# The last mixture of a two-layer kernel, computed with weight rows stationary instead of token rows

## The chip, the cores and the metric

The kernel is one program on one core of a Trainium2 chip. The metric is the device time of one execution in microseconds (us). Three executions of the kernel before took 1348.96, 1352.48 and 1351.76 us, median 1351.76.

## What is computed

A stream of 2048 tokens of 256 numbers (8 sequences of 256) goes through two layers. Each layer is a gated cross-attention to a short context and a gated mixture of experts. The change touches only the mixture of the second layer: 8 experts and a shared MLP of twice the width, so that 10 blocks of 176 hidden numbers (1760 in all) are computed for every token. The reference's second mixture comes down to this (its text is cut to what it computes; `combine` is zero for the experts that a token did not choose and one for the two shared blocks):

```python
xn = layernorm(x)                                   # [2048, 256]
p = softmax(xn @ gate_weight.T)                     # 8 experts
combine = where(p is among its row's two largest, p, 0), then two columns of 1
g, u = xn @ gate_rows.T, xn @ up_rows.T             # [2048, 1760] each
h = silu(g) * u * repeat(combine, 176, axis=1)
x = x + g_ffn[1] * (h @ down)                       # down [1760, 256]
```

The two products with `gate_rows` and `up_rows` are each made of three products of rounded halves (high by high, high by low, low by high), in the format fp32r.

## The kernel before

Tokens are handled in NG = 4 groups of G = 4 tiles of P = 128 tokens. The five engines run their own instruction lists and meet at semaphores. PSUM banks are used in rings of two: `q_ring` (products that VectorE reads), `s_ring` (products that ScalarE reads), `t_ring` (transposes and small products that ScalarE copies out), and the two `o_banks` for the final sums. A `fill` on TensorE waits until the bank's former content was read; a `read` waits until the bank is full.

The mixture of a group (`mixture` at lines 1214, 1527 and 1963 for VectorE, ScalarE and TensorE) works tile by tile:

- `gates_ups(j)` (products at line 1978): for each of 5 pairs of blocks, six products into an `s_ring` bank (gate) and six into a `q_ring` bank (up). The 128 tokens of the tile are stationary and 352 weight columns move. That is 60 products a tile and 240 a group.
- ScalarE applies Silu to each gate bank (line 1536, `sg`), 128 by 352. VectorE multiplies `sg`, the up bank and the token's combine weight in one instruction for each block (line 1208). Since tokens lie on the partitions, the combine weight is a scalar for each partition.
- `down(j)`: the 1760 hidden numbers lie along the free axis, so 14 transposes (line 1989) bring them onto partitions, four ScalarE copies (line 1541, `attnT`) take them out of PSUM, and 14 fp32 products of 256 columns (line 1997) sum them against `dn1` in one `o_bank`. Each such product appears in the trace as two instructions. `residual` (line 648) adds the sum to x.

TensorE's order in a group is gates_ups 0, gates_ups 1, down 0, gates_ups 2, down 1, gates_ups 3, the front of the next group, down 2, down 3. The front (`mixture_front`) transposes the next group's normalized tokens (line 1611), waits for ScalarE's four copies (lines 1449 and 1450), and computes the 8 gate logits (line 1876). VectorE's `gating` (lines 1187 to 1198) makes the combine weights from the logits. In its middle it waits for an exponential of ScalarE (line 1458). It runs after the last tile's multiplications. Groups 0 to 2 are one hardware loop, group 3 stands behind it. When all is done, SyncE stores the whole x (2 MB) at line 454.

Of the kernel before, what the change touches and what calls it, by code (L numbers as in the profile page):

```python
# [6 lines left out]
F32R = mybir.dt.float32r  # L7
I32 = mybir.dt.int32
ACT = mybir.ActivationFunctionType
ALU = mybir.AluOpType  # L10
# [18 lines left out]
W1 = (E1 + 2) * F1  # L29
# [72 lines left out]
def flamingo(nc, a, out, stages=4):  # L102
    with ExitStack() as ctx:
# [3 lines left out]
        def sem(name):  # L107
# [93 lines left out]
        gu_hi = sb("gu_hi", [P, 2 * G * ROW + 2 * NA * G * DIM + T // 2 + 2 * DIM], F32R)[:, 0:C * 5 * 4 * F1].rearrange(  # L201
            "p (c e g n) -> p c e g n", c=C, e=5, g=2)
# [17 lines left out]
        gu1 = sb("gu1", [P, C, 5, 2, 2 * F1], scope=loaded)  # L220
        loaded.close()
        gu_lo = sb("gu_lo", [P, C, 5, 2, 2 * F1], F32R)
        dn1 = sb("dn1", [P, FC, DIM])
        gate1 = sb("gate1", [P, C, E1])
        sg = sb("sg", [P, 2, 2 * F1])
        combine_w = sb("combine_w", [P, G, E1 + 2])
        act_v = soft[:].rearrange("p j n -> p (j n)")[:, 0:2 * FC * P].rearrange("p (b n) -> p b n", b=2)
# [13 lines left out]
        xnT_hi, xnT_lo = (xnT_split[:, n * C * G * P:(n + 1) * C * G * P].rearrange("p (c t) -> p c t", c=C)  # L241
                          for n in range(2))
# [89 lines left out]
        gate_exp = sem("gate_exp")  # L332

# [19 lines left out]
        QM, SM, TM, TMF = 20, 20, 20, 4  # L353
# [4 lines left out]
        def _(sp):  # L358
# [86 lines left out]
            sp.dma_start(gu1[:], a["L1_gu"].rearrange("(c p) e g n -> p c e g n", p=P)).then_inc(w4_loaded, 16)  # L445
# [5 lines left out]
            with sp.Fori(1, NG - 1) as i:  # L451
                next_context(i)
            sp.wait_ge(x_done, 1)
            sp.dma_start(out_d, x[:]).then_inc(stored, 16)
            sp.wait_ge(stored, 16)

        @block.gpsimd
        def _(pool):
# [99 lines left out]
            key_blocks(NG - 1)  # L558

        @block.vector  # L560
        def _(dve):
# [514 lines left out]
            def split_weights(p):  # L1076
                dve.wait_ge(w_rounded, p + 1)
                dve.tensor_tensor(gu_lo[:, :, p], gu1[:, :, p], gu_hi[:, :, p], ALU.subtract).then_inc(w_split, 1)

            def split_xn(i):  # L1080

                dve.wait_ge(xn_rounded, i + 1)
                dve.tensor_tensor(xnT_lo, xnT[:], xnT_hi, ALU.subtract).then_inc(xn_split, 1)
# [92 lines left out]
            GATE_CHAIN = 5 + 6  # L1176

            def gating(i):
# [7 lines left out]
                dve.wait_ge(t_ring.free, T5 + TMF - 8 + TM * i)  # L1186
# [12 lines left out]
                ch.wait()  # L1199

            def products(i, j):

                for p in range(5):
                    dve.wait_ge(s_ring.free, S5 + SM * i + 5 * j + p + 1)
                    b = qr.read(dve)
                    for e in range(2):
                        at = (2 * p + e) * F1
                        ins = dve.scalar_tensor_tensor(  # L1208
                            out=act_v[:, j % 2, at:at + F1], in0=sg[:, (j + p) % 2, e * F1:(e + 1) * F1],
                            scalar=combine_w[:, j, 2 * p + e:2 * p + e + 1], in1=b[:, e * F1:(e + 1) * F1],  # L1210
                            op0=ALU.mult, op1=ALU.mult)
                    ins.then_inc(q_ring.free, 1)

            def mixture(i, last):
                ch.at(MIX_BASE + MIX_CHAIN * i)
                qr.at(Q5, QM, i)
                products(i, 0)
                if not last:
                    row_stats(i + 1)
                products(i, 1)  # L1220
                if not last:
                    row_roots(EPS0)
                residual(3 * NG + i, 0, i, 3)
                if not last:

                    row_apply(i + 1)
                products(i, 2)
                residual(3 * NG + i, 1, i, 3)
                products(i, 3)
                if not last:  # L1230
                    split_xn(i + 1)
                    gating(i + 1)
                residual(3 * NG + i, 2, i, 3)
                residual(3 * NG + i, 3, i, 3)
                assert last or ch.k == MIX_CHAIN, ch.k
# [8 lines left out]
            with dve.Fori(0, NG - 1) as i:  # L1244
                mixture(i, False)
            mixture(NG - 1, True)
# [3 lines left out]
        def _(act):  # L1250
# [195 lines left out]
            def mixture_front():  # L1446
                for c in range(C):
                    b = tr.read(act)
                    act.activation(xnT_hi[:, c, :], b[:], ACT.Copy)
                    act.activation(xnT[:, c, :], b[:], ACT.Copy).then_inc(t_ring.free, 1)  # L1450
# [9 lines left out]
            def attention(i, last):  # L1460
# [18 lines left out]
                def round_weights(p):  # L1479
                    act.activation(gu_hi[:, :, p], gu1[:, :, p], ACT.Copy).then_inc(w_rounded, 1)  # L1480
# [3 lines left out]
                if last:  # L1484
                    mixture_front()
                    act.wait_ge(w4_loaded, 64)
# [39 lines left out]

            def mixture(i, last):
                sr.at(S5, SM, i)
                tr.at(T5 + TMF, TM, i)

                def silu(j):
                    for p in range(5):
                        b = sr.read(act)

                        act.wait_ge(q_ring.free, Q5 + QM * i + 5 * j + p - 1)
                        act.activation(sg[:, (j + p) % 2, :], b[:, 0:2 * F1], ACT.Silu).then_inc(s_ring.free, 1)  # L1536

                def act_out(j):
                    for g in range(4):
                        n = min(4, FC - 4 * g)  # L1540
                        act.activation(attn_flat[:, 4 * g:4 * g + n, :], tr.read(act)[:, 0:n * P].rearrange(  # L1541
                            "p (f t) -> p f t", f=n), ACT.Copy).then_inc(t_ring.free, 1)

                silu(0)
                silu(1)
                act_out(0)
                silu(2)
                act_out(1)
                silu(3)
                if not last:  # L1550
                    mixture_front()
                act_out(2)
                if not last:
                    gate_exponential(i + 1)
                act_out(3)

            attn_flat = attnT[:].rearrange("p b f t -> p (b f) t")
            gate_exponential(0)
            with act.Fori(0, NG - 1) as i:
                mixture(i, False)  # L1560
            mixture(NG - 1, True)

        @block.tensor
        def _(pe):
# [399 lines left out]

            def mixture(i, last):
                qr.at(Q5, QM, i)
                sr.at(S5, SM, i)
                tr.at(T5 + TMF, TM, i)

                def gates_ups(j):  # L1970
                    for p in range(5):
                        for o, (ring, end) in enumerate(((s_ring, sr), (q_ring, qr))):
                            b = end.fill(pe)

                            terms = [(v, w, c) for c in range(C) for v, w in (
                                (xnT_hi, gu_hi), (xnT_hi, gu_lo), (xnT_lo, gu_hi))]
                            for n, (v, w, c) in enumerate(terms):
                                mm = pe.matmul(b[:, 0:2 * F1], v[:, c, j * P:(j + 1) * P], w[:, c, p, o, :],  # L1978
                                               start=(n == 0), stop=(n == len(terms) - 1))
                            mm.then_inc(ring.full, 1)  # L1980

                def down(j):

                    pe.wait_ge(q_ring.free, Q5 + QM * i + 5 * (j + 1))
                    for g in range(4):
                        b = tr.fill(pe)
                        for f in range(4 * g, min(4 * g + 4, FC)):
                            n = min(P, W1 - f * P)
                            mm = pe.transpose(b[0:n, (f % 4) * P:(f % 4 + 1) * P],  # L1989
                                              act_v[:, j % 2, f * P:f * P + n], ident[:])  # L1990
                        mm.then_inc(t_ring.full, 1)
                    pe.wait_ge(o_read, G * (3 * NG + i) + j + 1)
                    for f in range(FC):
                        n = min(P, W1 - f * P)
                        if f % 4 == 0:
                            tr.evacuated(pe, 4 - f // 4)
                        mm = pe.matmul(o_banks[j % 2][:, 0:DIM], attn_flat[0:n, f, :], dn1[0:n, f, :],  # L1997
                                       start=(f == 0), stop=(f == FC - 1))
                    mm.then_inc(o_full, 1)

                pe.wait_ge(xn_split, i + 1)
                gates_ups(0)
                gates_ups(1)
                down(0)
                gates_ups(2)
                down(1)
                gates_ups(3)
                if not last:
                    mixture_front(i + 1)
                down(2)  # L2010
                down(3)

            attn_flat = attnT[:].rearrange("p b f t -> p (b f) t")
# [45 lines left out]
```

## Time and profile before

| what | value |
|---|---|
| executions | 1348.96, 1352.48, 1351.76 us (median 1351.76) |
| the profiled execution | 1348.91 us, its span 1347.2 us |
| mean granted TensorE clock over the span | 0.833 |
| TensorE products, busy share of the span | 77% |
| VectorE, ScalarE, GpSimd, busy share | 53%, 32%, 22% |
| stretch of the last mixture | 1034.4 to 1338.7 us |
| VectorE busy in it | about a third of each group or less |

The span runs from the first to the last instruction; the time of the execution is 1.7 us longer. The profile lists for each engine when it was busy, what ended its idle times, and the chain of work that ended last. Durations of matmuls overlap their neighbours in the record, so what a product costs is read from the distance between starts, or from the chain, and not from its own duration. The granted clock is 1.00 at 2.4 GHz and 0.50 at 1.2 GHz.

### The profile page before, as it was taken

The numbers are of one execution on the slowest core, as the hardware profiler recorded it, in microseconds if no ns is written. First come the engines' busy times: TensorE is split into PE (matmuls) and PEld (weight loads), VectorE is DVE, ScalarE is ACT, GpSimd is POOL, SyncE is SP. The second block draws the span as 40 slices with busy tenths as digits, with TensorE's granted clock in tenths as the row PEclk, the third lists the DMA queues.
The fourth block names the chain that finished last, engine by engine and source line by source line (L and its number), as shares of the span: only waits on it lengthen the run. The fifth ranks groups of instructions, "written<-read, shape, count | busy, mean of one in ns | idle before, by whom it ended". The sixth has DMA issues, their size and how long they took to land. (4 is left out here: it accounts for less than half of the span.)

```text
span 1347.2 us, 16347 instructions
## 1 busy us (share of the span) xinstructions
PE 1040.4 (77%) x5301; PEld 860.9 (64%) x5301; DVE 714.3 (53%) x1663; ACT 428.9 (32%) x789; POOL 296.6 (22%) x231
## 2 busy tenths in 40 slices
PE   5989989999766500866775447878879999999997
PEld 3857858678554300755665226564757989899896
DVE  6367586674768896222222488575865424242221
ACT  4555365544623100111111032323252232322321
POOL 0414223133000001788787120120200000000000
PEclk9999999999877655877778666767676999999999
DMA  7004000000001140788886620000000000000001
GB/s 264 3 0 136 1 1 1 0 1 1 0 0 39 42 108 22 168 182 175 170 175 113 191 107 1 2 0 0 0 0 0 1 1 0 0 0 0 0 0 63
DMA packets 59495, 66.39 MB, mean 49 GB/s; under 512 B 5565, under 2 KB 56247, under 8 KB 58679
## 3 DMA queue, kind: packets, MB, share of 16 engines
q1 hardware_dynamic: 45796, 46.52, 11.1%
q0 software_dynamic: 12288, 18.88, 7.9%
q8 instruction: 28, 0.46, 0.1%
q10 hardware_dynamic: 1363, 0.37, 0.1%
q14 instruction: 20, 0.16, 0.0%
HBM read 48.16 MB, written 17.56 MB: 49 GB/s over the span
## 5 line engine op out<-in xcount | busy, mean ns | idle before, releaser
L1978 PE MATMUL bank<-gu_hi,xnT_split 128*128 128x352 f32 x640 | 159.4, 329 | 0.0
L476 POOL TENSOR_TENSOR q_lo<-soft,q_hi 128x512 fp32r<-128x512 f32 x64 | 93.1, 1455 | 238.0 <-ACT soft L1338 237.8
L1978 PEld LDWEIGHTS bank<-gu_hi,xnT_split 128*128 128x128 f32 x640 | 113.4, 191 | 1.0 <-issue 0.7
L487 POOL DMA_INDIRECT xg<-table,src_now x64 | 63.9, 999 | 217.6 <-DVE src_now L948 198.5
L497 POOL DMA_INDIRECT acc<-y,dst_now x64 | 102.2, 1596 | 26.7 <-issue 20.6
L1978 PE MATMUL bank<-gu_lo,xnT_split 128*128 128x352 f32 x320 | 104.2, 326 | 0.0
L1208 DVE SCALAR_TENSOR_TENSOR soft<-sg,combine_w,bank 128x176 f32<-128x176 f32 x160 | 56.5, 394 | 88.1 <-PE bank L1978 82.3
L1997 PE MATMUL bank<-dn,attnT 128*128 128x256 f32 x448 | 102.1, 387 | 0.0
L1997 PEld LDWEIGHTS bank<-dn,attnT 128*128 128x128 f32 x448 | 86.1, 195 | 11.5
L728 DVE COPY qT<-bank 128x512 f32<-128x512 f32 x64 | 44.2, 690 | 89.3 <-PE bank L1683 88.2
L1536 ACT ACTIVATE sg<-bank 128x352 f32<-128x352 f32 x80 | 37.1, 464 | 153.0 <-PE bank L1978 153.0
L1783 PEld LDWEIGHTS bank<-xgT,w_gu 128*88 128x88 f32 x512 | 81.2, 205 | 7.1 <-issue 3.8
L1783 PE MATMUL bank<-xgT,w_gu 128*88 128x128 f32 x512 | 83.7, 333 | 0.7 <-issue 0.7
L648 DVE SCALAR_TENSOR_TENSOR x<-bank,gates,x 128x256 f32 (+1 forms) x48 | 22.8, 482 | 115.1 <-PE bank L1997 95.6
L968 DVE TENSOR_SCALAR y<-bank,xg 128x256 f32<-128x256 f32 x64 | 28.0, 479 | 96.5 <-PE bank L1796 79.2
L1769 PE MATMUL bank<-ident,xg 128*128 128x128 f32 x128 | 25.6, 333 | 59.4 <-DMA xg<-table,src_now 59.4
L1334 ACT ACTIVATE q_hi<-qT 128x512 fp32r<-128x512 f32 x64 | 40.4, 631 | 93.1 <-DVE qT L728 93.0
L1638 PE MATMUL bank<-vw,attnT 128*128 128x256 f32 x256 | 61.5, 395 | 4.2 <-ACT attnT L1288 4.2
L1668 PE MATMUL bank<-kT,qT 128*128 128x64 f32 x512 | 64.0, 268 | 0.0
L1668 PEld LDWEIGHTS bank<-kT,qT 128*128 128x128 f32 x512 | 62.5, 191 | 1.5
L1978 PEld LDWEIGHTS bank<-gu_lo,xnT_split 128*128 128x128 f32 x320 | 61.0, 191 | 0.3
L1769 PEld LDWEIGHTS bank<-ident,xg 128*128 128x128 f32 x128 | 17.9, 171 | 64.4 <-DMA xg<-table,src_now 54.1
(255 smaller groups left out, 2165.4 us busy)
## 6 DMA issues: line engine op xcount, KB each, us to landing
w_gu<-in_L_ffn_w_gu SPq DMA_DIRECT2D x32, 352.0 KB
w_dn<-in_L_ffn_w_down SPq DMA_DIRECT2D x32, 176.0 KB
acc<-zeros SPq DMA_DIRECT2D x2, 2176.0 KB, 12.0
acc_rows<-acc SPq DMA_DIRECT2D x8, 512.0 KB, 4.9
gu<-in_L_gu SPq DMA_DIRECT2D x1, 3520.0 KB, 13.3
table<-xw SPq DMA_DIRECT2D x4, 640.0 KB
wo<-in_L_xattn_Wo SPq DMA_DIRECT2D x2, 1024.0 KB, 15.7
wq<-in_L_xattn_Wq SPq DMA_DIRECT2D x1, 2048.0 KB, 18.0
```

Of the source, the lines that this page charges most:

```text
L476: pool.tensor_tensor(q2_lo[:, h % 3, :], q2[h % 2], q2_hi[:, h % 3, :], ALU.subtract).then_inc(q2_split, 1)
L487: pool.indirect_dma_start(xg[:, q, e, :], None, table, bass.IndirectOffsetOnAxis(ap=src_now[:, q, e:e + 1], axis=0)).then_inc(xg_loaded[q] ...
L497: pool.indirect_dma_start(acc[e], bass.IndirectOffsetOnAxis(ap=dst_now[:, q, e:e + 1], axis=0), y[:, q, e, :], None, compute_op=ALU.add).t ...
L728: dve.tensor_copy(qT[:, h % 3, :], qr.read(dve)[:]).then_inc(q_ring.free, 1)
L1208: ins = dve.scalar_tensor_tensor(out=act_v[:, j % 2, at:at + F1], in0=sg[:, (j + p) % 2, e * F1:(e + 1) * F1], scalar=combine_w[:, j, 2 * ...
L1334: act.activation(q2_hi[:, h % 3, :], qT[:, h % 3, :], ACT.Square)
L1638: mm = pe.matmul(o_banks[0][:, 0:DIM], attnT[:, j % 2, p, :], vw[:, j // 2, p, :], start=(p == 0), stop=(p == 7))
L1668: mm = pe.matmul(s_bank[0][:, at:at + SKV], qT[:, h % 3, j * P:(j + 1) * P], kT[:, h, (j // 2) * SKV:(j // 2 + 1) * SKV], start=True, stop ...
L1769: mm = pe.transpose(b[:, at:at + P], xg[:, q, e, c * P:(c + 1) * P], ident[:])
L1783: mm = pe.matmul(b[0:I0, e * P:(e + 1) * P], w_gu[:, q, e, c, o:o + I0], xgT[:, q % 2, e, c, :], start=(c == 0), stop=(c == C - 1))
L1978: mm = pe.matmul(b[:, 0:2 * F1], v[:, c, j * P:(j + 1) * P], w[:, c, p, o, :], start=(n == 0), stop=(n == len(terms) - 1))
L1997: mm = pe.matmul(o_banks[j % 2][:, 0:DIM], attn_flat[0:n, f, :], dn1[0:n, f, :], start=(f == 0), stop=(f == FC - 1))
```

## The change

The second mixture's products are turned around. A group is no longer worked tile by tile but in FC = 14 pieces of 128 hidden rows (the last has 96). For each piece `gate_up(f)` on TensorE makes

- one product of `chooser` (20 rows, the piece's 128 columns, stationary) with `combine_T` (20 rows, 512 tokens moving) into a `q_ring` bank: the combine weight of each hidden row's block, for each token. The 20 rows are the ten combine weights, rounded, and their ten remainders;
- six products into an `s_ring` bank and six into a `q_ring` bank with 128 weight rows stationary and 512 tokens moving.

ScalarE applies Silu to 128 by 512. VectorE multiplies twice over 512 columns, `sg` by the spread combine weights and then by the up bank. The result already has hidden rows on partitions. `down(f)` needs no transposes and is four products of 256 columns, one for each tile, into halves of the two `o_banks`, summed over the 14 pieces. TensorE runs gate_up(f) and then down(f - 1). The front of the next group stands after piece 6. `gating` stands on VectorE after piece 9, with its exponential on ScalarE after the Silu of piece 10. Two operations behind `gating` split the combine weights, and `combine_across` with `combine_in` transpose them for the next group. For group 0 these stand ahead of its first product. `xnT_hi` and `xnT_lo` have two buffers, GpSimd builds `chooser` after its last work, the loops over the groups are written out, and SyncE stores x in four parts of 512 KB as groups end.

```diff
+            def combine_across(i):
+                pe.wait_ge(combine_split, i + 1)
+                for half in range(2):
+                    b = tr.fill(pe)
+                    for k in range(2):
+                        mm = pe.transpose(b[0:2 * NW, k * P:(k + 1) * P], combine_2[:, 2 * half + k, :], ident[:])
+                    mm.then_inc(t_ring.full, 1)
+
             def mixture(i, last):
-                def gates_ups(j): ...
-                def down(j): ...
+                def gate_up(f):
+                    n, at = min(P, W1 - f * P), slice(f * P, min(f * P + P, W1))
+                    pe.matmul(qr.fill(pe)[0:n], chooser[:, at], combine_T[:], start=True,
+                              stop=True).then_inc(q_ring.full, 1)
+                    for g, (ring, end) in enumerate(((s_ring, sr), (q_ring, qr))):
+                        b = end.fill(pe)
+                        terms = [(w, v, c) for c in range(C) for w, v in (
+                            (gu_hi, xnT_hi), (gu_lo, xnT_hi), (gu_hi, xnT_lo))]
+                        for k, (w, v, c) in enumerate(terms):
+                            mm = pe.matmul(b[0:n], w[:, c, g, at], v[i % 2][:, c, :], start=(k == 0),
+                                           stop=(k == len(terms) - 1))
+                        mm.then_inc(ring.full, 1)
+                def down(f):
+                    pe.wait_ge(q_ring.free, Q5 + QM * i + 2 * f + 2)
+                    if f == 0:
+                        pe.wait_ge(o_read, 2 + 3 * NT + G * i)
+                    n = min(P, W1 - f * P)
+                    for j in range(G):
+                        mm = pe.matmul(o_banks[j // 2][:, j % 2 * DIM:(j % 2 + 1) * DIM],
+                                       act_v[0:n, f % 2, j * P:(j + 1) * P], dn1[0:n, f, :],
+                                       start=(f == 0 and j % 2 == 0), stop=(f == FC - 1 and j % 2 == 1))
+                        if f == FC - 1 and j % 2:
+                            mm.then_inc(o_full, 2)
+                tr.evacuated(pe)
                 pe.wait_ge(xn_split, i + 1)
+                for f in range(FC):
+                    gate_up(f)
+                    if f:
+                        down(f - 1)
+                    if f == 6 and not last:
+                        mixture_front(i + 1)
+                if not last:
+                    combine_across(i + 1)
+                down(FC - 1)
 # VectorE
+                ch.add(dve.tensor_copy(combine_2[:, :, 0:NW].bitcast(F32R), combine_w[:]))
+                ch.wait()
+                dve.tensor_tensor(combine_2[:, :, NW:2 * NW], combine_w[:], combine_2[:, :, 0:NW],
+                                  ALU.subtract).then_inc(combine_split, 1)
+            def products(i, f):
+                n, v = min(P, W1 - f * P), act_v[:, f % 2, :]
+                dve.wait_ge(s_ring.free, S5 + SM * i + f + 1)
+                dve.tensor_tensor(v[0:n], sg[0:n, f % 2, :], qr.read(dve)[0:n], ALU.mult).then_inc(q_ring.free, 1)
+                qr.evacuated(dve)
+                dve.tensor_tensor(v[0:n], v[0:n], qr.read(dve)[0:n], ALU.mult).then_inc(q_ring.free, 1)
+                for f in range(FC):
+                    products(i, f)
+                    if not last:
+                        ...
+                        elif f == 8:
+                            split_xn(i + 1)
+                        elif f == 9:
+                            gating(i + 1)
+                mixture_out(i)
 # ScalarE
+                for f in range(FC):
+                    n, b = min(P, W1 - f * P), sr.read(act)
+                    act.wait_ge(q_ring.free, Q5 + QM * i + 2 * f - 3)
+                    act.activation(sg[0:n, f % 2, :], b[0:n], ACT.Silu).then_inc(s_ring.free, 1)
+                    if not last:
+                        if f == 6:
+                            mixture_front(i + 1)
+                        elif f == 10:
+                            gate_exponential(i + 1)
+                if not last:
+                    combine_in()
 # SyncE
+            for i in range(NG):
+                sp.wait_ge(o_read, 2 + 3 * NT + G * (i + 1))
+                sp.dma_start(out_d[:, G * i:G * (i + 1), :], x[:, G * i:G * (i + 1), :]).then_inc(stored, 16)
             sp.wait_ge(x_done, 1)
-            sp.dma_start(out_d, x[:]).then_inc(stored, 16)
-            sp.wait_ge(stored, 16)
+            sp.wait_ge(stored, 16 * NG)
```

## Rows read from the trace of the kernel before

**Rows 1.** Stretches of groups 1 and 3 and the end: busy, clock, DMA

```profile
1114.20:1190.80 76.60, 74.05 (x433) 69.53 (x433) 25.48 (x81) 22.45 (x45) 0.00 (x0) 0.98 0.00 0
...
1267.90:1338.70 70.80, 69.74 (x408) 65.16 (x407) 16.07 (x45) 17.10 (x36) 0.00 (x0) 1.00 0.00 1
1338.70:1347.20 8.50, 0.00 (x0) 0.00 (x0) 0.46 (x1) 0.00 (x0) 0.00 (x0) 0.79 0.74 247
```

**Rows 2.** Chain that ended last, end of group 1: start, us, what

```profile
1159.16 9.60 PE bank L1978 x60
...
1171.43 2.18 PE bank L1876 x16
1173.61 3.05 PE bank L1989 x14
...
1182.71 0.45 PE bank L1989 x4
...
1184.76 6.05 PE bank L1997 x28
```

**Rows 3.** Timeline of TensorE, layer 0 queries, six fp32r products of 512 columns

```profile
211.97 0.39 PE L1683 MATMUL bank<-xnT_rest,wq_hi 128*128 128x512 f32 x1
...
213.13 0.28 PE L1659 MATMUL bank<-q_hi,band_r 128*16 128x256 f32 x1
...
213.59 1.00 PE L1668 MATMUL bank<-kT,qT 128*128 128x64 f32 x8
```

**Rows 4.** Timeline around a product with one row stationary, full clock

```profile
968.83 0.29 PEld L1924 LDWEIGHTS bank<-bo,ones 1*128 1x128 f32 x2 [0.33 <-issue]
968.83 0.69 PE L1924 MATMUL bank<-bo,ones 1*128 1x256 f32 x2
969.45 0.20 PEld L1915 LDWEIGHTS bank<-ident,c 128*128 128x128 f32 x2 [0.33 <-issue]
```

**Rows 5.** Timeline around products with 16 rows stationary

```profile
80.67 1.45 PE L1574 MATMUL bank<-wk,ctxK 128*128 128x512 f32 x3
...
82.05 0.32 PEld L1701 LDWEIGHTS bank<-ident,n_rows 16*128 16x128 f32 x4 [0.76 <-issue]
```

**Rows 6.** Timeline of ScalarE and VectorE in the gating of group 1

```profile
1099.17 1.28 ACT L1458 ACT_TABLE_LOAD   x1
1100.46 0.23 ACT L1458 ACTIVATE gate_s<-gate_s 128x32 f32<-128x32 f32 x1
1100.72 0.18 DVE L1191 TENSOR_REDUCE gate_s<-gate_s 128x4 f32<-128x32 f32 x1 [3.76 <-ACT gate_s L1458]
...
1103.77 0.19 DVE L1198 TENSOR_TENSOR combine_w<-gate_s 128x32 f32<-128x32 f32 x1
```

**Rows 7.** Groups by line: busy us, mean ns, idle before

```profile
L1536 ACT ACTIVATE sg<-bank 128x352 f32<-128x352 f32 x79 | 36.7, 464 | 153.0 <-PE bank L1978 153.0
L1541 ACT ACTIVATE attnT<-bank 128x512 f32<-128x512 f32 x48 | 27.0, 595 | 36.2 <-PE bank L1989 36.2
...
L728 DVE COPY qT<-bank 128x512 f32<-128x512 f32 x64 | 44.2, 690 | 89.3 <-PE bank L1683 88.2
```

**Rows 8.** Timeline before and at the start of the last mixture

```profile
1030.05 0.69 PE L1915 MATMUL bank<-ident,c 128*128 128x128 f32 x2
...
1030.77 0.38 ACT L1476 ACTIVATE c1T<-bank 128x256 f32<-128x256 f32 x1 [5.86 <-PE bank L1915]
...
1038.76 0.19 DVE L1198 TENSOR_TENSOR combine_w<-gate_s 128x32 f32<-128x32 f32 x1
```

**Rows 9.** Stretches of lower clock: busy, granted clock (third from the end)

```profile
1034.40:1039.30 4.90, 4.90 (x18) 4.90 (x18) 3.88 (x15) 1.98 (x3) 0.00 (x0) 0.50 0.00 0
...
1171.00:1176.00 5.00, 4.57 (x28) 4.31 (x28) 1.60 (x3) 1.81 (x5) 0.00 (x0) 0.70 0.00 0
```

**Rows 10.** DMA issues: size, median us from issue to landing

```profile
out<-x SPq DMA_DIRECT2D x1, 2048.0 KB, 7.5
...
cand<-cand SPq DMA_DIRECT2D x1, 32.0 KB, 1.8
```

More of the change, by code:

```diff
@@ L28 @@
 E1, F1 = 8, 176
-W1 = (E1 + 2) * F1
+NW = E1 + 2
+W1 = NW * F1
 FC = -(-W1 // P)
@@ L240, in flamingo @@
         xnT_split = sb("xnT_split", [P, QK * D1 + C * G * P], F32R)
-        xnT_hi, xnT_lo = (xnT_split[:, n * C * G * P:(n + 1) * C * G * P].rearrange("p (c t) -> p c t", c=C)
-                          for n in range(2))
+        xnT_other = sb("xnT_other", [P, 2 * C * G * P], F32R)
+        xnT_hi, xnT_lo = ([v[:, n * C * G * P:(n + 1) * C * G * P].rearrange("p (c t) -> p c t", c=C)
+                           for v in (xnT_split, xnT_other)] for n in range(2))
         qk1_stat = sb("qk1_stat", [P, 2, QK])
@@ L332, in flamingo @@
         gate_exp = sem("gate_exp")
+        chooser_step = sem("chooser_step")
+        chooser_ready = sem("chooser_ready")
+        combine_split = sem("combine_split")
         x_d = a["x"].rearrange("b t d -> (b t) d").rearrange("(n p) d -> p n d", p=P)
@@ L558, in _ @@
             key_blocks(NG - 1)
+            blank = sg[:].rearrange("p b n -> p (b n)")[0:2 * NW, 0:NW // 2 * F1].rearrange(
+                "p (e n) -> p e n", e=NW // 2)
+            for half in range(2):
+                if half:
+                    pool.wait_ge(chooser_ready, half)
+                pool.memset(blank, 0.0).then_inc(chooser_step, 1)
+                for part_ in range(2):
+                    pool.wait_ge(chooser_step, 3 * half + part_ + 1)
+                    pool.affine_select(out=blank, in_=blank, compare_op=ALU.not_equal, fill=1.0,
+                                       base=-NW // 2 * half - NW * part_, pattern=[[-1, NW // 2], [0, F1]],
+                                       channel_multiplier=1).then_inc(chooser_step, 1)
+                pool.wait_ge(chooser_step, 3 * half + 3)
+                pool.tensor_copy(chooser[:, half * NW // 2 * F1:(half + 1) * NW // 2 * F1].rearrange(
+                    "p (e n) -> p e n", e=NW // 2), blank).then_inc(chooser_ready, 1)
         @block.vector
@@ L1199, in gating, with mixture_out @@
                 ch.wait()
[L1201 to L1212, printed above, removed]
+                ch.add(dve.tensor_copy(combine_2[:, :, 0:NW].bitcast(F32R), combine_w[:]))
[8 more added lines that the diff above has]
+                dve.tensor_tensor(v[0:n], v[0:n], qr.read(dve)[0:n], ALU.mult).then_inc(q_ring.free, 1)
+            def mixture_out(i):
+                for j in range(G):
+                    dve.wait_ge(o_full, G * (3 * NG + i) + 2 * (j // 2 + 1))
+                    xj = x[:, G * i + j, :]
+                    dve.scalar_tensor_tensor(out=xj, in0=o_banks[j // 2][:, j % 2 * DIM:(j % 2 + 1) * DIM],
+                                             scalar=gates[:, 3:4], in1=xj, op0=ALU.mult,
+                                             op1=ALU.add).then_inc(o_read, 1)
             def mixture(i, last):
@@ L1216, in mixture @@
                 qr.at(Q5, QM, i)
[L1217 to L1234, printed above, removed]
+                for f in range(FC):
+                    products(i, f)
+                    if not last:
+                        if f == 1:
+                            row_stats(i + 1)
+                        elif f == 2:
+                            row_roots(EPS0)
+                        elif f == 3:
+                            row_apply(i + 1)
+                        elif f == 8:
[3 more added lines that the diff above has]
+                mixture_out(i)
                 assert last or ch.k == MIX_CHAIN, ch.k
@@ L1243, in _ @@
             dve.wait_ge(o_read, 2 + 3 * NT)
-            with dve.Fori(0, NG - 1) as i:
-                mixture(i, False)
-            mixture(NG - 1, True)
+            for i in range(NG):
+                mixture(i, i == NG - 1)
             dve.drain().then_inc(x_done, 1)
@@ L1525, in _, with combine_in @@
             attention(NG - 1, True)
+            def combine_in():
+                for half in range(2):
+                    act.activation(combine_T[:, half * 2 * P:(half + 1) * 2 * P], tr.read(act)[0:2 * NW, 0:2 * P],
+                                   ACT.Copy).then_inc(t_ring.free, 1)
             def mixture(i, last):
                 sr.at(S5, SM, i)
[L1529 to L1549, printed above, removed]
-                if not last:
[L1551 to L1557, printed above, removed]
+                for f in range(FC):
[7 more added lines that the diff above has]
+                            gate_exponential(i + 1)
+                if not last:
+                    combine_in()
             gate_exponential(0)
-            with act.Fori(0, NG - 1) as i:
-                mixture(i, False)
-            mixture(NG - 1, True)
+            tr.at(T5 + TMF)
+            combine_in()
+            for i in range(NG):
+                mixture(i, i == NG - 1)
         @block.tensor
@@ L1967, in mixture @@
                 sr.at(S5, SM, i)
[L1968 to L1999, printed above, removed]
@@ new lines, in down @@
+                def down(f):
[3 more added lines that the diff above has]
+                    n = min(P, W1 - f * P)
+                    for j in range(G):
+                        mm = pe.matmul(o_banks[j // 2][:, j % 2 * DIM:(j % 2 + 1) * DIM],
[3 more added lines that the diff above has]
+                            mm.then_inc(o_full, 2)
@@ L2014, in _ @@
+                down(FC - 1)
             pe.wait_ge(w_split, 5)
-            with pe.Fori(0, NG - 1) as i:
-                mixture(i, False)
-            mixture(NG - 1, True)
+            pe.wait_ge(chooser_ready, 2)
+            tr.at(T5 + TMF)
+            combine_across(0)
+            for i in range(NG):
+                mixture(i, i == NG - 1)
 _INS = ["x", "ctx_1024", "g_xattn", "g_ffn", "L0_xattn_Wq", "L0_xattn_Wk", "L0_xattn_Wo",
```

52 lines of the change are left out of this document (24 added, 28 removed).

## Prediction, made before the changed kernel ran

> **What bounds the kernel now.** I read the busy stretches first, then the chain that ended last, then timelines at the places where the chain changes. In the stretches [rows 1] the reader sees TensorE busy for 74.05 of 76.60 us in group 1 and for 69.74 of 70.80 us in group 3, VectorE for 25.48 and 16.07. So the last mixture, 1034.4 to 1338.7 us, goes by what TensorE executes plus the few places where it waits. The chain says what that is [rows 2]. One tile's 60 gate and up products take 9.60 us, 0.160 each. One `down` takes 2.05 us from its first transpose (1182.71) to its first real product (1184.76), with a wait for ScalarE in it, and then 6.05 us for 14 products in 28 passes, 0.216 a pass. The front of the next group, from the end of the 60 products (1168.76) to the next transposes (1173.61), takes 4.85 us. Four tiles give 4 x (9.60 + 2.05 + 6.05) = 70.8 us, which is group 3, and the front with its slow clock makes 76.6 us of it in group 1. The sum closes, so each of these terms may be exchanged for a new one.
>
> **Removed.** The transposes, with their ScalarE wait: 16 tiles x 2.05 = **-32.8 us** [rows 2].
>
> **Unchanged.** `down` has 56 products of 256 columns a group before and after. The passes of 0.216 us are as many. The front stays as it is.
>
> **The pieces.** A group has 14 x 12 = 168 products with 512 moving columns in place of 240 with 352. The same kind of product stands in the layer 0 queries [rows 3]: from 211.97 to 213.13 lie five of them, 0.232 us each. 672 x 0.232 = 155.6 us against 960 x 0.160 = 153.6: **+2.0 us**. The gain of wider products is nothing; columns set the price (86016 against 84480 a group).
>
> **The spreading product, streaming.** 14 a group with 512 columns: 56 x 0.232 = **+13.0 us**. That only 20 rows are used makes it no shorter: the passes over one row in [rows 4] are no shorter than those over 128 (below).
>
> **The spreading product, its breaks.** Here I look at products whose stationary operand has few rows, among others of 128. In [rows 4] a product over one row begins at 968.83 and the next one's weights at 969.45: 0.62 us for two passes of 256 columns that take 0.43 us in [rows 2]. So 0.19 us is lost. The weight load's idle time ahead of it reads "issue": nothing that the trace shows kept it from being loaded under the matmuls before, as all others are. It began only when these had ended. It is the same on the way in (0.33 us of idle ahead of both). In [rows 5] the products with 16 rows do it too: three matmul passes from 80.67 at 0.43 us each end at 81.96, and the load follows at 82.05, with its own 0.1 us still to come. In [rows 3] the change from 16 columns to 128 (213.13 to 213.59, four passes of 0.115) costs nothing, so it is the rows that do it and not the columns. The chooser has 20 rows, close to 16, and stands alone between products of 128 rows, so it has a break on either side: 2 x 56 x 0.2 = **+22.4 us**. Bounds: 0 if 20 rows behave like 128, and 0.3 us each at the lower clock. I take the 16-row and 1-row value, as 20 is nearest to 16.
> The Trainium skill, page "TensorE: Matmul & The Clock Gate", section "LDWEIGHTS (loading the stationary operand)", says that a load goes by its columns, so that 32 rows take as long as 128. It knows no break, and by it this term would be 0 and the sum +1.8 us. The durations of the loads agree with it, the idle time before them does not, and I go by the latter; the first rival is the page's case.
>
> **The start.** Now TensorE begins the products at 1034.4, while VectorE is still gating until 1038.95 [rows 8], and it runs 4.9 us at clock 0.50 [rows 9]. In the changed kernel the two splitting operations come first (2 x 0.22, to 1039.4), then two transposes (0.69 for two, [rows 8]), then two copies of 0.38 with a hop each, and only then `tr.evacuated` lets the pieces begin: about 1041.0, **+6.6 us**. I let the slow stretch of 4.9 us move with it (bounds: not there, -2.5; twice as long, +2.5). In groups 1 to 3 the four transposes lie in TensorE's list for 0.6 us each time, and the copies hide under down(13), 1.7 us: **+1.9 us**.
>
> **The gating.** This is a new wait, in the middle of a group. VectorE stands in `gating` after piece 9, and queued behind it is its multiplication of piece 10, which alone frees the bank for the spreading product of piece 11. `gating` waits in its middle for an exponential that stands behind the Silu of piece 10. Counted from the end of the gate product of piece 10: Silu 0.07 + 0.60 (464 ns for 352 columns, 595 for a copy of 512, [rows 7]), table load 1.28, exponential 0.23, hop 0.03, VectorE's chain from 1100.72 to 1103.96 = 3.24, the two new operations 0.44, the multiplication 0.03 + 0.69 (a 512 column read of PSUM, [rows 7]), hop 0.06: 6.67 us [rows 6]. In that time TensorE has up(10), 6 x 0.232, and down(9), 8 x 0.216: 3.12 us. It stands still for 3.55 us, in three groups: **+10.7 us**. In the kernel before this chain lay beside down(2).
>
> **The clock.** After a pause the clock falls: the front's wait for four ScalarE copies is followed by 5 us at 0.70 [rows 9], which is 3 us at the lower level and 1.5 us of lost work. The front keeps its own. The gating's pause is longer, so I give it one such loss a group: **+4.5 us** (bounds 0, and two spells each of 1.7, 10.2).
>
> **The rest.** Piece by piece VectorE and ScalarE are covered. Silu ends 0.67 and the first multiplication 1.4 us after the gate product, the second 2.1; TensorE needs the first bank after 1.39 + 1.73 = 3.1 us, and down of the piece some 3 us later. row_stats, row_roots, row_apply and split_xn each fit in the 3 us that a piece leaves on VectorE (row_roots, the longest, is 12 small operations at the 0.22 us steps of [rows 6], 2.6 us); if that cover were gone, each would cost what it is longer than it. GpSimd builds `chooser` after its last work of layer 1, in layer 1's last attention group, with nothing queued behind it; if TensorE came first it would wait at `chooser_ready`. The written-out loops and the second buffers I cost at 0. The end: now the last sum ends at 1338.65, and 8.5 us follow [rows 1], with the 2 MB store landing after 7.5 [rows 10]. After the change two `x` additions in a row (0.5 us more) and a 512 KB store, between 1.8 (32 KB) and 7.5 us, by proportion of size 3.2: **-3.8 us** (bounds -5 and +0.5).
>
> **Sum.** -32.8 + 2.0 + 13.0 + 22.4 + 6.6 + 1.9 + 10.7 + 4.5 - 3.8 = **+24.5 us**. From the profiled execution's own 1348.9 that is 1373.4; from the median of the runs, 2.9 higher, 1376.3. I predict **1375**. What I call the same below is within 0.3%, 4 us, about what a measurement of this kernel can tell from none.
>
> **Rivals.**
> *The chooser has no breaks* (20 rows are handled as 128, or its load is pulled under the passes of down). For it: the 96-row products among the 28 passes of `down` show none (0.216 a pass with them, [rows 2]). Against it: all rows with 1 and 16 rows show one. Sum +2.1, time 1351 to 1354, not slower by what can be told. The point at which it decides is a break of 0.02 us: 112 x 0.02 = 2 us carries the sum over 4 us. Chance 0.12.
> *A product's price is its weight load, not its columns*: a load lasts 0.19 us, and 352 columns run at 0.160. If 512 ran at 0.160 too, 728 products would save 0.072 each, -52 us, time 1323, faster. Against it, [rows 3] have exactly this product at 0.232. Chance 0.02. The Trainium skill, same page, section "Back-to-back issue gap", gives about 131 ns for 512 columns in a stream with loads; by it 728 x 0.1 = 73 us less, 1302. The trace disagrees.
> *The clock falls more often*: each gating pause brings two slow spells and the start stays slow twice as long: +5.7 + 2.5, time 1383. For it: the pause is twice the front's; against it, the front costs one spell. Chance 0.10.
> *As worked out*: 0.76, with its own range 1362 to 1385.
>
> **How the numbers follow.** Low end: forecast from 1348.9 with no clock losses at start and pauses and the best store, 1373.4 - 2.5 - 4.5 - 1.2 = 1365, less a few us for breaks of 0.15: 1361. High end: 1376.3 + 8.2 = 1385, with a dearer store 1387. Outside lie the two cases with chances 0.12 and 0.02 and a few in a hundred above. Faster by over 0.3%: 0.02 from the second, 0.02 from the first and 0.01: 0.05. Same: 0.07, nearly all of the first. Slower: 0.88.
>
> **What would show it.** The last product at about 1367 in the span (1338.7 + 24.5 + 3.8). Weight loads of the chooser and of the first gate product with idle time "issue" ahead of each, 0.62 us from chooser start to gate start; a piece of 5.1 us (4.7 without breaks). Pieces of six products at 0.232. No transposes of `soft`. The first piece at 1041. In groups 0 to 2 one TensorE pause of 3.5 us before piece 11, ended by VectorE's multiplication, with a lower clock after it. Group 3 of about 72 us against 70.8, groups 1 and 2 of about 84 against 76.6. A group 3 of 66 us would show the break term wrong; pauses at other pieces would show the cover of VectorE wrong.

## The result and the profile after

The changed kernel took 1377.38 us (median of 4 runs, 1373.94 to 1378.16) beside 1350.36 us for the kernel before (median of 4). The ratio is 1.0206, with a 95% interval of 1.0184 to 1.0228: 27 us slower. The forecast was 24.5 us slower, 1375 us, and 1377.38 lies in the stated range of 1361 to 1387. The profiled execution took 1378.16 us with a span of 1376.3.

The first view is the busy stretches of the four groups and the chain, as in [rows 1] and [rows 2]. Columns: stretch, length, busy time of TensorE's products, its weight loads, VectorE, ScalarE, GpSimd, then granted clock, DMA share and GB/s.

```profile
1041.00:1125.50 84.50, 79.33 (x305) 60.07 (x305) 28.43 (x67) 14.33 (x24) 0.00 (x0) 0.89 0.00 1
1125.50:1211.00 85.50, 80.32 (x327) 60.78 (x326) 30.93 (x72) 14.25 (x25) 0.00 (x0) 0.94 0.02 7
1211.00:1298.00 87.00, 81.81 (x331) 62.15 (x330) 30.54 (x71) 14.39 (x26) 0.00 (x0) 0.92 0.02 6
1298.00:1370.90 72.90, 72.88 (x301) 54.76 (x300) 21.05 (x33) 8.89 (x16) 0.00 (x0) 1.00 0.02 8
```

The last group has no front, no gating and no lower clock, and the transposes of `soft` are gone from it. It is still longer than the last group before (72.9 against 70.8). TensorE is busy for 94% of each of the first three and for all of the last, VectorE for 34 to 36% and 29%, so TensorE sets the pace as before.

Pieces are numbered from 0 to 13 in each group. The chain, start and length in us, shows what a piece is made of:

```profile
1072.15 0.42 PE bank L1998
1072.57 2.97 PE bank L2005 x12
1075.54 1.73 PE bank L2016 x8
```

The spreading product is line 1998, the gate and up products line 2005, down line 2016. A piece takes 5.12 us. The timeline of weight loads at the same place (start, us, engine, line) answers to [rows 4] and [rows 5]:

```profile
1072.08 0.18 PEld L1998 LDWEIGHTS bank<-combine_T,chooser 20*128 20x128 f32 x1 [0.33 <-issue]
1072.08 0.49 PE L1998 MATMUL bank<-combine_T,chooser 20*128 20x512 f32 x1
1072.50 0.19 PEld L2005 LDWEIGHTS bank<-xnT_split,gu_hi 128*128 128x128 f32 x1 [0.24 <-issue]
1072.61 0.19 PEld L2005 LDWEIGHTS bank<-xnT_split,gu_lo 128*128 128x128 f32 x1
1072.84 0.42 PEld L2005 LDWEIGHTS bank<-xnT_split,gu_hi 128*128 128x128 f32 x2
```

Only the load of the 20-row chooser and its successor have idle time named issue ahead of them; from the third load on, one starts every 0.23 us, under the product before. The chooser's load began at 1072.08, only when the last pass of down had ended, although VectorE had read its bank by 1070.40 (a multiplication of 0.69 us from 1069.71). From its start to that of its successor lie 0.42 us for a product that streams in 0.23.

The pause in the middle of groups 0 to 2, in the chain:

```profile
1102.36 0.59 issue
1102.95 1.28 ACT L1486
1104.24 0.24 ACT gate_s L1486
...
1107.78 0.20 DVE combine L1226
...
1108.12 0.69 DVE soft L1235
...
1108.85 0.79 PE bank L1998
1109.64 5.24 PE bank L2005 x12
1114.88 1.73 PE bank L2016 x8
```

This is the gating as the prediction counted it from [rows 6]: Silu of piece 10 (the 0.59 us that the chain names issue), table load, exponential, VectorE's chain, the multiplication, and only then the spreading product of piece 11. The 12 products behind it take 5.24 us instead of 2.97. TensorE's own waits in the last mixture say the same (engine, line, whom it waited for: total us, times, longest):

```profile
PE bank L1998 <- DVE soft L1235: 10.3, 3, 3.5
PE bank L1989 <- DVE combine L1228: 5.2, 1, 5.2
PE bank L1894 <- ACT xnT L1478: 5.2, 3, 1.7
PE bank L1998 <- ACT combine_T L1558: 0.5, 1, 0.5
```

### The profile page after: what moved, and what is told of

It reads as the page before. It is cut to its first block and busy times, and to the rows that moved or that the text cites. A ratio compares the mean times of both kernels' runs of the same rounds, so it can differ in the third digit from the quotient of the medians.

```text
span 1376.3 us, 14873 instructions
## 1 busy us (share of the span) xinstructions
PE 1057.9 (77%) x4861; PEld 817.6 (59%) x4861; DVE 738.5 (54%) x1623; ACT 396.6 (29%) x709; POOL 303.8 (22%) x239
## 5 line engine op out<-in xcount | busy, mean ns | idle before, releaser
L1235 DVE TENSOR_TENSOR soft<-sg,bank 128x512 f32<-128x512 f32 (+1 forms) x56 | 38.5, 688 | 182.5 <-ACT sg L1566 177.0
L507 POOL DMA_INDIRECT acc<-y,dst_now x64 | 102.2, 1596 | 26.3 <-issue 19.1
L2016 PE MATMUL bank<-dn,soft 128*128 128x256 f32 (+1 forms) x448 | 105.9, 380 | 0.0
L1566 ACT ACTIVATE sg<-bank 128x512 f32<-128x512 f32 (+1 forms) x56 | 33.5, 599 | 249.3 <-PE bank L2005 249.3
L2016 PEld LDWEIGHTS bank<-dn,soft 128*128 128x128 f32 (+1 forms) x448 | 85.3, 191 | 13.6
L2005 PE MATMUL bank<-xnT_split,gu_hi 128*128 128x512 f32 (+1 forms) x224 | 84.8, 442 | 0.0
L1801 PE MATMUL bank<-xgT,w_gu 128*88 128x128 f32 x512 | 80.8, 326 | 0.7 <-issue 0.7
L2005 PE MATMUL bank<-xnT_other,gu_hi 128*128 128x512 f32 (+1 forms) x224 | 80.5, 421 | 0.0
L1656 PEld LDWEIGHTS bank<-vw,attnT 128*128 128x128 f32 x256 | 49.7, 197 | 13.7 <-ACT attnT L1316 6.6
L2005 PEld LDWEIGHTS bank<-xnT_split,gu_hi 128*128 128x128 f32 (+1 forms) x224 | 46.5, 208 | 18.4 <-issue 7.7
L1924 PE MATMUL bank<-v_blocks,attnT 128*128 (+1 forms) x256 | 51.0, 370 | 8.0 <-DVE x L1098 7.9
```

Source lines behind the costliest of these rows:

```text
L507: pool.indirect_dma_start(acc[e], bass.IndirectOffsetOnAxis(ap=dst_now[:, q, e:e + 1], axis=0), y[:, q, e, :], None, compute_op=ALU.add).t ...
L1656: mm = pe.matmul(o_banks[0][:, 0:DIM], attnT[:, j % 2, p, :], vw[:, j // 2, p, :], start=(p == 0), stop=(p == 7))
L1801: mm = pe.matmul(b[0:I0, e * P:(e + 1) * P], w_gu[:, q, e, c, o:o + I0], xgT[:, q % 2, e, c, :], start=(c == 0), stop=(c == C - 1))
L1924: mm = pe.matmul(o_banks[j % 2][:, 32 * p:32 * (p + 1)], attnT[:, j % 2, p, :], v_blocks[:, i % 2, j // 2, p].rearrange("p o d -> p (o d)" ...
L2005: mm = pe.matmul(b[0:n], w[:, c, g, at], v[i % 2][:, c, :], start=(k == 0), stop=(k == len(terms) - 1))
L2016: mm = pe.matmul(o_banks[j // 2][:, j % 2 * DIM:(j % 2 + 1) * DIM], act_v[0:n, f % 2, j * P:(j + 1) * P], dn1[0:n, f, :], start=(f == 0 an ...
```

## The experiments

All kernels are the changed one with the edits shown. In each set the kernel before ran beside them; its median was 1351.83 us in the first set (runs 1 to 4) and 1351.79 us in the second (5 to 8). Every kernel computes the whole output.

**Run 1: 128 rows in the spreading product.**

```diff
-        chooser = sb("chooser", [2 * NW, W1], F32R)
-        combine_T = sb("combine_T", [2 * NW, G * P], F32R)
+        KR = 128
+        chooser = sb("chooser", [KR, W1], F32R)
+        combine_T = sb("combine_T", [KR, G * P], F32R)
...
                 pool.memset(blank, 0.0).then_inc(chooser_step, 1)
+                if not half:
+                    pool.wait_ge(chooser_step, 1)
+                    pool.tensor_copy(combine_T[:], sg[0:KR, 0, :]).then_inc(rest_zero, 1)
+                    pool.wait_ge(rest_zero, 1)
```

> The changed kernel, with chooser and combine_T made of 128 rows instead of 20, the added 108 rows zero. Nothing else of the work changes: the product streams the same 512 columns. Theory (a stationary operand of few rows among ones of 128 is not loaded under the matmuls ahead of it, and neither is its successor): the two breaks of 0.2 us a piece go, a piece takes 4.74 us instead of 5.13, 56 pieces give -22 us, 1377.4 becomes about 1355.5, and the idle time named issue ahead of the loads of the chooser and of the first gate product is gone. Rival (the break comes from the single product of another operand with its own waits, whatever its rows): no change, 1377.

Measured: 1351.65 us (10 runs), ratio to before 0.9999, interval 0.9988 to 1.0011. More multiplications by zero took 25.7 us away, and the kernel is level with the one before, although the three gating pauses are still in it. A timeline of a piece in this kernel:

```profile
1300.92 0.19 PEld L2004 LDWEIGHTS bank<-combine_T,chooser 128*128 128x128 f32 x1
1300.95 0.58 PE L2004 MATMUL bank<-combine_T,chooser 128*128 128x512 f32 x1
1301.14 0.19 PEld L2011 LDWEIGHTS bank<-xnT_other,gu_hi 128*128 128x128 f32 x1
...
1305.65 0.19 PEld L2004 LDWEIGHTS bank<-combine_T,chooser 128*128 128x128 f32 x1
```

The issue idle is gone and a piece takes 4.73 to 4.76 us (1300.92 to 1305.65). The theory holds and the rival falls: the product is as alone as before and waits for the same things. What this edit can't tell apart is which operand matters: the rows of the weights and of the tokens' side grow together. The spans differ by 26.3 us (1376.3 and 1350.0), more than the 22 expected. Of the rest 3.6 us are clock: the piece behind each gating pause lasts 6.2 us against 4.75 for its neighbours, an excess of 1.45 us; in the changed kernel that excess is 2.6, 3.0 and 2.5 us. The clock over 9 us from the pause's end on, first in the changed kernel and then in run 1:

```profile
1108.80:1117.80 9.00, 8.95 (x26) 6.55 (x27) 2.06 (x3) 0.60 (x1) 0.00 (x0) 0.68 0.00 0
```

```profile
1103.40:1112.40 9.00, 8.90 (x32) 7.25 (x33) 2.14 (x5) 1.19 (x2) 0.00 (x0) 0.81 0.00 0
```

A mean of 0.68 is 5.8 us at the lower level, 0.81 is 3.4 us. With the breaks the lower clock lasted longer, after all three pauses. Runs 4 and 5 below repeat it: the piece behind the pause takes 7.85, 8.18 and 7.61 us with 64 rows, which break, and 6.19, 6.20 and 6.19 with 96, which don't. So it goes with the breaks in all four kernels; why it does is not shown.

**Run 2: the exponential ahead of the Silu of piece 10.**

```diff
-                        elif f == 10:
+                        elif f == 9:
                             gate_exponential(i + 1)
```

> The changed kernel, with ScalarE's exponential of the gating placed ahead of the Silu of piece 10 instead of behind it (one number changed). Theory: VectorE's gating no longer waits for the gate product of piece 10, its chain ends 6.4 us after the gate product of piece 9 and the multiplication of piece 10 is done about 1 us before TensorE needs its bank. The pause of 3.45 us in three groups goes, and with it the lower clock behind it (the 12 products after it took 5.2 us instead of 3.0): 3 x (3.45 + 2.3) = -17 us, about 1360. Rival (the clock loss belongs to the front and comes anyway): -10 us, 1367. Second rival (the gating's own length, 3.7 us, pauses TensorE wherever it stands): under -4 us.

Measured: 1358.32 us (7 runs), ratio 1.0051, interval 1.0033 to 1.0069. The span is 1355.9, 20.4 us shorter than that of the changed kernel. TensorE's waits in the last mixture are now only these:

```profile
PE bank L1989 <- DVE combine L1228: 5.2, 1, 5.2
PE bank L1894 <- ACT xnT L1478: 5.2, 3, 1.7
PE bank L1998 <- ACT combine_T L1558: 0.5, 1, 0.5
```

All three pauses are gone, 10.5 us by the starts of the pieces, and with them the lower clock behind them: pieces 10 and 11 take 5.12 us like the others, 8.0 us less in sum for piece 11. That is 18.5 of the 20.4 us. Another 1.5 us is the front of the third group, whose two pieces take 16.4 us here and 17.9 in the changed kernel, by a shorter lower clock that the edit didn't aim at. The theory holds; both rivals, -10 and under -4, fall. The gating itself fits in a piece; it was the exponential's place in ScalarE's list that did not.

**Run 3: both edits.** 

> Both edits together, 128 rows and the exponential ahead of piece 10. Theory: the two are separate terms of a TensorE-bound stage and add up, 1377.4 - 22 - 17 = 1338, 12 us faster than the kernel before. Rival: with shorter pieces (4.74 us) VectorE's gating no longer fits and a part of the pause comes back, 1342 to 1345.

Measured: 1338.78 us (4 runs), ratio 0.9911, interval 0.9882 to 0.9941. Pieces 9 to 11 take 4.73 to 4.76 us in every group, so no part of the pause comes back and the rival falls. The terms add up, and with 128 rows and one number changed the transposed form is faster than the kernel before by 13 us.

**Run 4: 64 rows** (as run 1 with `KR = 64`). 

> As the first of these runs but with 64 rows, 44 of them zero. It tells which number of rows makes the break. If only up to 32 rows break: a piece of 4.74 us and about 1355. If anything other than the full height breaks: a piece of 5.13 us and 1377 (but the 96-row products in down show no break, so half-way behaviour such as one break of two would be seen as 4.9 us and 1366).

Measured: 1382.46 us, one run. The loads show both breaks:

```profile
1322.77 0.18 PEld L2004 LDWEIGHTS bank<-combine_T,chooser 64*128 64x128 f32 x1 [0.33 <-issue]
1322.77 0.50 PE L2004 MATMUL bank<-combine_T,chooser 64*128 64x512 f32 x1
1323.19 0.19 PEld L2011 LDWEIGHTS bank<-xnT_other,gu_hi 128*128 128x128 f32 x1 [0.24 <-issue]
```

A piece takes 5.13 us, as with 20 rows. That the time is 4.3 us above the changed kernel's profiled execution (1378.16) is not the rows: the attention products that precede the last mixture begin 3.4 us later in this execution (1033.97 against 1030.55), and from the first spreading product to the end of the span both take the same, 336.3 and 335.8 us.

**Run 5: 96 rows** (`KR = 96`). 

> The changed kernel with 96 rows in the spreading product (76 of them zero). 20 and 64 rows showed the breaks, 128 none, and the 96-row products among the 128-row ones in down show none. Theory (what counts is whether a stationary operand takes more than half of the array's rows): no break, a piece of 4.75 us, 1350 to 1356. Rival (everything under 128 breaks where the moving format is fp32r): 5.13 us a piece, 1375 to 1382.

Measured: 1351.49 us, one run, a span of 1349.7.

```profile
1310.06 0.19 PEld L2004 LDWEIGHTS bank<-combine_T,chooser 96*128 96x128 f32 x1
1310.09 0.58 PE L2004 MATMUL bank<-combine_T,chooser 96*128 96x512 f32 x1
...
1314.81 0.19 PEld L2004 LDWEIGHTS bank<-combine_T,chooser 96*128 96x128 f32 x1
```

No break, 4.75 us a piece. Between 64 and 96 rows the behaviour changes. Each number of rows has one execution, but a break would show in each of its 56 pieces. The rival that anything under 128 rows breaks falls.

**Run 6: the spreading product last in its piece**, on top of run 3. In group 0 its first one, and the transposes of the combine weights, now stand behind 12 products.

```diff
 def gate_up(f):
-    pe.matmul(qr.fill(pe)[0:n], chooser[:, at], combine_T[:], ...).then_inc(q_ring.full, 1)
     for g, (ring, end) in enumerate(((s_ring, sr), (q_ring, qr))):
         ...
+    if f == 0:
+        if i == 0:
+            combine_across(0)
+        tr.evacuated(pe)
+    pe.matmul(qr.fill(pe)[0:n], chooser[:, at], combine_T[:], ...).then_inc(q_ring.full, 1)
```

> 128 rows and the early exponential as in the run of both, and the spreading product moved behind the gate and up products of its piece, so that group 0 begins its first 12 products while VectorE is still gating. Theory (the start was worth 6.6 us because TensorE stood still behind the combine weights): the 12 products at the lower clock, 5.2 us, fit into the 6.7 us of waiting, 1338.8 becomes about 1334. Rival (VectorE's first multiplication now waits for the up products, so the spread bank comes free later): no gain, and pieces longer than 4.75 us.

Measured: 1334.27 us (4 runs), ratio 0.9874, interval 0.9848 to 0.9900: 4.5 us under run 3, as expected. Run 3 ran in the other set and the intervals of the two ratios overlap at their ends (0.9882 to 0.9900), so the mechanism is read from the trace: the first product starts at 1034.53, right behind the attention, and the 12 products (5.42 us in the chain) end at about the time when VectorE's gating does:

```profile
1034.53 0.80 PE L2009 MATMUL bank<-xnT_split,gu_hi 128*128 128x512 f32 x1
...
1039.39 0.20 DVE L1234 TENSOR_TENSOR combine<-combine_w,combine 128x40 f32<-128x40 f32 x1
...
1041.17 0.50 PE L2016 MATMUL bank<-combine_T,chooser 128*128 128x512 f32 x1 [0.51 <-ACT combine_T L1564]
```

The number agrees better than its parts. From the end of the attention (1032.09 in run 3, 1034.60 here) to the end of the span the gain is 6.4 us. The start gives about 3.3 of it: piece 2 begins 12.9 us after the attention and not 16.2. The 5.2 us expected are not reached, in part because TensorE now waits 0.8 us for VectorE's first multiplication, which comes behind ScalarE's table load of 1.28 us (1041.14) and the first Silu. The steps from one group to the next give about 1, and the third front 1.6, its two pieces taking 15.7 us instead of 17.3 by a shorter lower clock. The attention that ends 2.5 us later takes some back. Runs 7 and 8 below differ by this same edit inside one set: 5.3 us.

**Run 7: the front cut in two**, on top of run 3.

```diff
 # TensorE
-                    if f == 6 and not last:
-                        mixture_front(i + 1)
+                    if f == 6 and not last:
+                        transpose_only(i + 1)
+                    if f == 7 and not last:
+                        tr.evacuated(pe)
+                        logits_front()
 # ScalarE
                         if f == 6:
                             mixture_front(i + 1)
+                        elif f == 7:
+                            logits_in()
```

> 128 rows and the early exponential, and the front of the next group cut in two: its transposes stay behind piece 6, its logit products stand behind piece 7, so that ScalarE's four copies lie beside the products of piece 7. Theory (the lower clock after the front follows from TensorE's pause of 1.8 us): the two pieces around the front took 17.3 us instead of 9.5 in the run of both and will take about 12.5, 3 x 4.8 = -14, 1338.8 becomes about 1325. Rival (the small transposes and logit products bring the lower clock by themselves): only the pause is saved, -6, about 1333.

Measured: 1323.40 us (4 runs), ratio 0.9797, interval 0.9773 to 0.9821: 15.4 us under run 3. The two pieces around the front take 12.3 us in all three groups, instead of 17.3. The chain around the front, in run 3 and then in this run:

```profile
1072.00 0.45 PE bank L1635 x4
...
1072.47 0.60 ACT xnT_other L1483
...
1074.59 2.89 PE bank L1900 x16
1077.48 0.63 PE bank L2004
1078.11 4.71 PE bank L2011 x12
```

```profile
1072.89 0.87 PE bank L1908 x8
1073.77 0.23 PE bank L2021
1074.00 2.80 PE bank L2028 x12
1076.80 1.73 PE bank L2039 x8
1078.53 1.68 PE bank L1917 x16
1080.21 0.33 PE bank L2021
1080.54 2.78 PE bank L2028 x12
```

In run 3 the pause for ScalarE's copies is followed by logit products of 2.89 us and 12 products of 4.71. Without the pause the same logit products take 1.68 and the 12 products 2.78, and the granted clock over this stretch is 1.00:

```profile
1060.00:1090.00 30.00, 30.00 (x147) 25.48 (x146) 10.11 (x18) 8.07 (x15) 0.00 (x0) 1.00 0.00 1
```

So the small products don't bring the lower clock by themselves, and the rival falls. That the pause does it is not shown as cleanly: the edit also parts the transposes from the logit products by a whole piece, and neither the two side by side without a pause nor a pause of 1.8 us among full products was tried. The gating's pause, 3.45 us among full products, does bring it (runs 1 and 2). The pause of 1.8 us with its small products around it cost 5 us a group, the pause included.

**Run 8: all four edits.** 

> All four edits: 128 rows, early exponential, spreading product last in its piece, front cut in two. Theory: the terms add up, 1338.8 - 4.5 - 14 = 1320, 31 us under the kernel before, ratio 0.977. Rival: 1328 if the clock falls at the front anyway.

Measured: 1318.11 us (5 runs, 1317.09 to 1319.07), ratio 0.9758, interval 0.9738 to 0.9779. This beats the kernel before by 33.7 us and the changed one by 59 us. The terms add up once more (expected 1320), and the rival at 1328 falls.

## Why the prediction was right

It held, and for its stated reasons; two of its terms, both of the clock, were 6.4 us too small together, and in part luck brought the number so close. The two profiled executions differ by 29.3 us (1378.16 and 1348.91), 4.8 more than the sum of 24.5. That the median lies only 2.4 us above the 1375 is because the kernel before was profiled in one of its faster executions, and because 1375 was set between the two starting points.

- *The breaks* (predicted 0.2 us each, 22.4 in all) decided the sign. Without them the forecast would have been +2.1 us. In the changed kernel a piece takes 5.13 us; less 12 x 0.231 for the gate and up products, 1.73 for down and 0.231 for the spreading product that leaves 0.40 us for two breaks, 22 us in all. Run 1 removed them, and the kernel was again level with the one before. The step from products with 1 and 16 rows [rows 4, 5] to one with 20 was sound; runs 4 and 5 put the limit between 64 and 96 rows. The rule of the Trainium skill, page "TensorE: Matmul & The Clock Gate", section "LDWEIGHTS (loading the stationary operand)", agrees with the duration of the load (0.18 us for 20 rows, 0.19 for 128). It says nothing of when a load may start, and a sum that goes by it alone misses these 22 us. (By that rule the prediction gave +1.8 us; its own terms without the breaks make +2.1.) One sign in the prediction was misworded: chooser start to gate start is 0.42 us, with the rest of the two breaks outside; 0.62 is both with the streaming.
- *Streaming* (+2.0 and +13.0): products of 512 columns start every 0.231 us. The second rival, 0.160 us, is out, and so is the 131 ns that the prediction cited from the Trainium skill.
- *The transposes* (-32.8): none is left in the chain. No run tried this term alone.
- *The start* (+6.6): chooser starts at 1040.48, predicted 1041.0, with the attention ending 0.7 us earlier in this execution. Run 6 took about 3.3 us of this term back.
- *The gating* (10.7): three pauses of 3.45 us, 10.3 in the waits. Run 2 removed them by moving one instruction.
- *The clock* was under-sized, in two places. Behind the gating's pauses it cost 8.0 us against 4.5, the lower clock lasting longer with the breaks than without (run 1: 4.4). The front was left "as it is", a term of nothing: in the kernel before it and its clock cost 6.3, 5.9 and 6.3 us in groups 0 to 2 (18.5, by the chain), and now pieces 6 and 7 exceed their plain length by 7.6, 6.1 and 7.7 us, 21.4 in all. The stretch of lower clock around it grew. Here is the front of group 0, first before and then after the change:

```profile
1091.70:1106.10 14.40, 12.36 (x68) 10.63 (x67) 5.27 (x15) 5.90 (x12) 0.00 (x0) 0.88 0.01 1
```

```profile
1077.30:1090.00 12.70, 10.98 (x46) 8.84 (x44) 1.38 (x2) 3.03 (x7) 0.00 (x0) 0.73 0.00 0
```

A mean of 0.88 over 14.4 us is 3.5 us at the lower level, 0.73 over 12.7 us is 6.9. Group 2 shows the same two numbers; in group 1 it is 3.3 before and 3.4 after (a mean of 0.85 over 11.2 us). Why it is long in two groups and short in one stays open. These two terms are 6.4 us too small (3.5 and 2.9). The attention that ends 0.65 us earlier and smaller pieces, crossings and pauses take 1.7 of it back: the last product was to end at about 1367.0 and ends at 1371.7 (down of the last piece, 1368.21 and 16 passes).
- *The end* (-3.8): from the last product to the end of the span 4.6 us instead of 8.55. The store lands in 2.9 us, predicted 3.2:

```profile
out<-x SPq DMA_DIRECT2D x4, 512.0 KB, 2.9
```

- *VectorE and ScalarE are covered*: TensorE waits for VectorE at piece 11 and at no other.
- The rival of more clock losses was thus in good part true: it gave 10.2 us to the gating's pauses, and the 8.0 measured lie nearer to that than to the 4.5 taken; the start stayed slow for about 6 us, not for twice 4.9.

## What to carry to other kernels

Look at weight loads with idle time named issue: a small product among full ones can cost more by its two breaks than by its columns, and padding its stationary operand with zero rows can be the cure. When a chain over two engines is moved to another place, follow the other engine's list too; here one exponential behind one Silu cost 19 us. A TensorE pause should be priced with the slower products behind it: behind pauses of 3.45 us they cost 1.5 to 3.0 us here, and around one of 1.8 us among small products about 3.

## What the runs showed of the hardware

- A product with 20 or 64 stationary rows between products of 128 rows delays its own weight load and the next one's until the passes ahead have ended, 0.2 us each at the full clock; with 96 or 128 rows the load lies under them (a piece of 5.13 us against 4.75, runs 1, 4 and 5).
- An fp32r product of 512 columns takes 0.231 us with 96 or 128 rows, zeros or not.
- The lower clock after a pause of 3.45 us lasted 3.4 us in a stream without breaks (run 1) and 5.8 us with them (the changed kernel, group 0). After a pause of 1.8 us and small products it slowed 12 products from 2.8 to 4.7 us (run 3). Without the pause, and with a piece between them, the same small products left the clock at 1.00 (run 7).
- On ScalarE the table load for the exponential took 1.28 us (1102.95 to 1104.24), and the exponential began as it ended.
